# A macaron block on one core: the shared experts' work moved into the expert-pair loop, the experts' first layers computed transposed

## The reference, cut to what matters

```python
x = x + 0.5 * ffn(layernorm(x))
x = x + attention(layernorm(x))
x = x + 0.5 * ffn(layernorm(x))
def ffn(x):                                   # xf: (4096, 128)
    scores = softmax(xf @ gate_w.T)           # 64 experts, 6 chosen per token
    _, idx = top_k(scores + gate_b, 6)
    # the first 64 choices that fall on an expert, in token order, get a slot: xb (64, 64, 128)
    h = silu(einsum('ecd,eid->eci', xb, w1)) * einsum('ecd,eid->eci', xb, w3)   # i = 88
    yb = einsum('eci,edi->ecd', h, w2)
    y = scatter_add(yb * weight)              # back to the tokens
    z = (silu(xf @ ws1.T) * (xf @ ws3.T)) @ ws2.T    # shared experts, 176 wide
    return y + z
```

## Time and profile before

| what | value |
|---|---|
| median of 3 runs | 614.8 us (612.43 to 616.04) |
| the profiled execution's span | 615.3 us, mean granted TensorE clock 0.726 |
| busy | PE 448.7 us (73%), PEld 298.5 (49%), DVE 356.6 (58%), ACT 223.2 (36%), POOL 333.6 (54%) |
| first pass: loop, tail | POOL scatters from 103.3 to 184.0, planes added from 194.2 |
| attention | about 230 to 404 |
| second pass: loop, tail | POOL scatters from 494.0 to 574.7, planes added from 584.3 to 612.1 |
| chain that ended last | PE 32%, DVE 30%, DMA 12%, issue 12%, ACT 7%, POOL 4% |

### The profile page before, as it was taken

The page is one execution under the profiler, slowest core; times in us unless marked ns, Lnnn a source line. Parts: engine busy times, 40 slices in busy tenths (PEclk is TensorE's granted clock), DMA queues, the critical chain, the costliest instruction groups (busy, mean ns, idle before and its releaser), DMA issues.

```text
span 615.3 us, 12760 instructions
## 1 busy us (share of the span) xinstructions
PE 448.7 (73%) x4788; PEld 298.5 (49%) x4788; DVE 356.6 (58%) x992; ACT 223.2 (36%) x509; POOL 333.6 (54%) x259
## 2 busy tenths in 40 slices
PE   1876965996699425799999979147877399957970
PEld 1823643553345313577777768146445255524440
DVE  6497981221113992687777865487999232212097
ACT  4732112332224268555555530184321133312420
POOL 6177786888886700322222220003877678888691
PEclk9987785555559755799999986558778555555995
DMA  7988500101008990001111110541000000100592
GB/s 256 387 243 317 230 8 7 11 5 11 6 5 314 410 368 1 1 3 38 35 34 35 34 36 10 161 173 52 2 0 8 8 8 6 10 6 7 166 410 108
DMA packets 34388, 60.39 MB, mean 98 GB/s; under 512 B 12611, under 2 KB 18846, under 8 KB 33870
## 3 DMA queue, kind: packets, MB, share of 16 engines
q1 hardware_dynamic: 23078, 58.41, 26.5%
q0 software_dynamic: 11264, 1.38, 2.5%
HBM read 37.43 MB, written 29.36 MB: 109 GB/s over the span
## 4 chain that ended last, share of the span: by engine, by line
PE 32%; DVE 30%; DMA 12%; issue 12%; ACT 7%; POOL 4%; another core or an unknown queue 1%; SPq 1%; DVEq 0%; POOLq 0%; ACTq 0%
DVE X L971 9%; DMA rows_d<-A 5%; PE bank L776 5%; PE bank L895 5%; PE bank L793 4%; PE bank L876 4%; PE bank L766 3%; PE bank L786 3%; ACT A L508 3%; DMA planes_d<-Bb,put_i 3%; DVE Cb L1074 2%; DVE bn L976 2%; DMA Bb<-planes_d 2%; POOL planes_d L438 2%; DVE A L1055 2%
## 5 line engine op out<-in xcount | busy, mean ns | idle before, releaser
L438 POOL DMA_INDIRECT planes_d<-Bb,put_i x64 | 100.4, 1569 | 26.1 <-issue 19.4
L452 POOL DMA_INDIRECT A<-rows_d,tok_i x64 | 71.4, 1116 | 20.1 <-issue 16.6
L1104 DVE TENSOR_TENSOR ring<-ring,bank 128x88 f32<-128x88 f32 x64 | 15.8, 246 | 107.2 <-ACT ring L574 77.4
L673 PE MATMUL bank<-ident,A 128*128 128x128 f32 x96 | 21.6, 399 | 54.4 <-ACT A L508 40.2
L479 POOL TENSOR_TENSOR Bb<-Cb,chm 128x576 f32<-128x576 f32 x16 | 19.0, 1221 | 67.1 <-DVE Cb L1138 33.7
L396 POOL TENSOR_TENSOR Bb<-Eb,st 128x512 f32<-128x512 f32 x8 | 8.9, 1112 | 79.3 <-DVE st L1022 79.3
L766 PE MATMUL bank<-ident,A 128*128 128x128 f32 x64 | 29.8, 465 | 29.4 <-DMA A<-rows_d,tok_i 23.5
L703 PE MATMUL bank<-XT,ws1s 128*88 128x512 f32 x64 | 41.4, 734 | 6.2 <-DVE Eb L1016 5.3
L568 ACT ACTIVATE ring<-bank 128x128 f32<-128x128 f32 x64 | 17.8, 278 | 77.6 <-PE bank L766 67.0
L673 PEld LDWEIGHTS bank<-ident,A 128*128 128x128 f32 x96 | 17.4, 212 | 57.3 <-issue 29.9
L479 POOL TENSOR_TENSOR Bb<-w3s,chm 128x576 f32<-128x576 f32 x16 | 17.9, 1148 | 49.2 <-PE bank L918 49.2
(11 more groups left out here) (155 smaller groups left out, 1108.3 us busy)
## 6 DMA issues: line engine op xcount, KB each, us to landing
planes_d<-zeros SPq DMA_DIRECT2D x8, 2048.0 KB, 20.9
w3s<-in_w3T SPq DMA_DIRECT2D x2, 2816.0 KB
rows_d<-A SPq DMA_DIRECT2D x8, 512.0 KB, 12.4
A<-planes_d SPq DMA_DIRECT2D x8, 512.0 KB, 9.5
PL<-planes_d SPq DMA_DIRECT2D x8, 512.0 KB, 10.2
Cb<-planes_d SPq DMA_DIRECT2D x8, 512.0 KB, 10.9
Bb<-planes_d SPq DMA_DIRECT2D x8, 512.0 KB, 12.0
w1s<-in_w1T SPq DMA_DIRECT2D x1, 2816.0 KB
```

Source lines behind the costliest of these rows:

```text
L438: pool.indirect_dma_start(out=planes_d[f], in_=Y[:, s, :], in_offset=None, out_offset=bass.IndirectOffsetOnAxis(ap=put_i[:, s:s + 1], axis=0),
L452: pool.indirect_dma_start(out=A[:, t, :], out_offset=None, in_=rows_d, in_offset=bass.IndirectOffsetOnAxis(ap=tok_i[:, t:t + 1], axis=0), ...
L673: ins = pe.transpose(bank[g % 2][:, (i % 4) * P:(i % 4 + 1) * P], A[:, i, :], ident[:, :])
```

## The change

The experts' first layers are computed transposed: the weights are now the stationary operand (88 columns), the gathered slots XBT the moving one (64 columns per expert), and the output is 88 x slots. With it go `g_turn`, ACT's `copy_gT` and one step of the loop's skew: the gated product is written by DVE straight to where `expert_out` reads it.

All shared-expert work moves into the loop: iterations s = 2 to 25 each do one part, `shared_hidden(g, 0)`, `shared_hidden(g, 1)` or `shared_out(g)`, for g from 0 to 7. Hidden layers use banks 1 and 6, the output bank 1 again. ACT applies Silu from bank 1; DVE, no longer POOL, multiplies with bank 6 read from PSUM, and adds half of the output to X itself. The matmul of twice X and the constant for it go.

In the tail DVE adds all four planes; POOL has nothing to do there.

```diff
-    EARLY = 4
-    BASE_AFTER = EARLY - 2
...
+        SH = [PL[0:I, 512 * k:512 * k + 512] for k in range(2)]
+        HS = [[PL[0:I, 1024 + 512 * (2 * j + k):1536 + 512 * (2 * j + k)] for k in range(2)] for j in range(2)]
...
-        SHARED = ((0, 1), (4, 5))
+        SHARED = (1, 6)
+
+        def shared_part(s):
+            n = s - 2
+            return divmod(n, 3) if 0 <= n < 3 * NSH else None
...
-                sp.wait_ge(z_added, NSH * f + EARLY)
+                sp.wait_ge(z_added, NSH * (f + 1))
...
-                for g in range(EARLY):
-                    shared_gates(g)
-                    if g == BASE_AFTER:
-                        counts()
+                counts()
...
-                def add_planes(g):
...
+                def shared_silu(g, k):
+                    n = (f * NSH + g) * 2 + k
+                    act.wait_ge(sh_ps, n + 1)
+                    if n >= 2:
+                        act.wait_ge(sh_gated, n - 1)
+                    act.activation(SH[k], bank[SHARED[0]][0:I, :], ACT.Silu).then_inc(sh_silu, 1)
...
-                    act.activation(SG[s % 2], bank[2 + s % 2][:, 0:I], ACT.Silu)\
-                        .then_inc(silu_done, 1)
...
+                    act.activation(SG[s % 2], bank[2 + s % 2][0:I, 0:P], ACT.Silu).then_inc(silu_done, 1)
+
+                for s in range(NS + 2):
                     if s < NS:
                         copy_xbT(s)
                     if 1 <= s <= NS:
                         silu(s - 1)
-                    if 2 <= s <= NS + 1:
-                        copy_gT(s - 2)
-                shared(EARLY, NSH)
+                    part = shared_part(s)
+                    if part and part[1] < 2:
+                        shared_silu(*part)
...
                 def shared_hidden(g, k):
                     n = (f * NSH + g) * 2 + k
-                    if g == 0 and k == 1:
-                        pe.wait_ge(shifted, NG * (f + 1))
-                    if g == EARLY:
-                        pe.wait_ge(y_sb, (f + 1) * NS)
-                    if g:
-                        pe.wait_ge(sh_copied, 2 * (n - 1))
-                    for w, bk in zip((ws1s, ws3s), SHARED[k]):
+                    if g == 0 and k == 0:
+                        looked_up(6)
+                    if n:
+                        pe.wait_ge(sh_gated, n)
+                    if k == 0 and (f or g):
+                        pe.wait_ge(z_added, f * NSH + g)
+                    for w, bk in zip((ws1s, ws3s), SHARED):
...
                 def shared_out(g):
-
                     n = f * NSH + g
-                    if n:
-                        pe.wait_ge(z_added, n)
-                    pe.matmul(bank[7][:, :], twice[:, :], X[:, 4 * g:4 * g + 4, :].rearrange("p i d -> p (i d)"),
-                              start=True, stop=False, skip_group_check=True)
                     pe.wait_ge(sh_gated, 2 * n + 2)
...
-                    for w, off in ((w1s, 0), (w3s, I)):
+                    for w, off in ((w1s, 0), (w3s, P)):
                         for k in range(2):
-                            ins = pe.matmul(bank[2 + s % 2][CAP * k:CAP * k + CAP, off:off + I], XBT[s % 2][:, CAP * k:CAP * k + CAP],
-                                            w[:, 2 * s + k, :], start=True, stop=True)
+                            cols = slice(off + CAP * k, off + CAP * k + CAP)
+                            ins = pe.matmul(bank[2 + s % 2][0:I, cols], w[:, 2 * s + k, :],
+                                            XBT[s % 2][:, CAP * k:CAP * k + CAP], start=True, stop=True)
...
-                for s in range(NS + 3):
+                for s in range(NS + 2):
                     if s < NS:
                         xb_turn(s)
                     if 1 <= s <= NS:
                         hidden(s - 1)
-                    if 2 <= s <= NS + 1:
-                        g_turn(s - 2)
-                    if s >= 3:
-                        expert_out(s - 3)
...
+                    if s >= 2:
+                        expert_out(s - 2)
+                    part = shared_part(s)
+                    if part and part[1] < 2:
+                        shared_hidden(*part)
+                    elif part:
+                        shared_out(part[0])
...
-                    for buf in PLANES[0:3]:
-                        if buf is PLANES[2]:
-                            dve.wait_ge(planes_added, NG * (n // 2) + g + 1)
+                    for buf in PLANES:
                         then(dve.tensor_tensor(xg, xg, buf[:, cols], ALU.add))
...
-                    dve.tensor_tensor(GA[s % 2], SG[s % 2], bank[2 + s % 2][:, I:2 * I], ALU.mult).then_inc(gated, 1)
+                        dve.wait_ge(y_ps, f * NS + s - 1)
+                    dve.tensor_tensor(GT[s % 2], SG[s % 2], bank[2 + s % 2][0:I, P:2 * P], ALU.mult).then_inc(gated, 1)
+
+                def shared_gate(g, k):
+                    n = (f * NSH + g) * 2 + k
+                    dve.wait_ge(sh_silu, n + 1)
+                    if g >= 2:
+                        dve.wait_ge(z_ps, f * NSH + g - 1)
+                    dve.tensor_tensor(HS[g % 2][k], SH[k], bank[SHARED[1]][0:I, :], ALU.mult).then_inc(sh_gated, 1)
+
+                def shared_add(g):
+                    xg = X[:, 4 * g:4 * g + 4, :].rearrange("p i d -> p (i d)")
+                    dve.wait_ge(z_ps, f * NSH + g + 1)
+                    dve.scalar_tensor_tensor(xg, bank[SHARED[0]][:, :], 0.5, xg, ALU.mult, ALU.add).then_inc(z_added, 1)
```

More of the change, by code:

```diff
@@ L106, in macaron_kernel @@
         plane0 = sb("plane0", [P, NS])
-        twice = sb("twice", [P, P])
         gate_s = sb("gate_s", [P, NE])
@@ L189, in macaron_kernel @@
         counts_ready = sem("counts_ready")
-        sh_copied = sem("sh_copied")
+        sh_silu = sem("sh_silu")
         group_ready = sem("group_ready")
@@ L361, in _ @@
             pool.memset(eps[:, :], LN_EPS).then_inc(ident_ready, 1)
-            then(pool.memset(twice[:, :], 0.0))
-            keep(twice[:, :], ALU.not_equal, 0, [[-1, P]], 1, 2.0)
             then(pool.memset(before[:, :], 1.0))
@@ L456, in _ @@
                     add(s)
-                def add_planes(g):
-                    cols = slice(g * GI * D, (g + 1) * GI * D)
-                    pool.wait_ge(part_in[g], 16 + 64 * (f + 1))
-                    pool.tensor_tensor(out=PLANES[2][:, cols], in0=PLANES[2][:, cols], in1=PLANES[3][:, cols],
-                                       op=ALU.add).then_inc(planes_added, 1)
-                for g in range(EARLY, NSH):
-                    if g >= NSH - 2:
-                        add_planes(g - (NSH - 2))
-                    shared_gates(g)
-                for g in range(2, NG):
-                    add_planes(g)
                 if f == 0:
@@ L716, in shared_out @@
                         for k in range(2):
-                            ins = pe.matmul(bank[7][:, i * D:(i + 1) * D], SHARED_BUFS[g >= EARLY][2][g % 2][k][:, i * P:(i + 1) * P], ws2s[:, k, :],
-                                            start=False, stop=(k == 1), skip_group_check=True)
+                            ins = pe.matmul(bank[SHARED[0]][:, i * D:(i + 1) * D], HS[g % 2][k][:, i * P:(i + 1) * P],
+                                            ws2s[:, k, :], start=(k == 0), stop=(k == 1))
                     ins.then_inc(z_ps, 1)
@@ L737, in look_up @@
                             ins.then_inc(look_ps, 1)
[L739 to L752 removed]
+                base()
                 look_up()
[L754 removed]
                 pe.wait_ge(w_in, 48 + 16 * f)
@@ L1109, in weigh @@
                                       ALU.mult, ALU.mult).then_inc(y_sb, 1)
-                for s in range(NS + 3):
+                for s in range(NS + 2):
                     if 1 <= s <= NS:
                         gate(s - 1)
-                    if s >= 3:
-                        weigh(s - 3)
+                    if s >= 2:
+                        weigh(s - 2)
+                    part = shared_part(s)
+                    if part and part[1] < 2:
+                        shared_gate(*part)
+                    elif part:
+                        shared_add(part[0])
             ffn(0)
```

84 lines of the change are left out of this document (7 added, 77 removed).

## The result

The changed kernel took 628.1 us, median of 4 runs (626.25 to 632.96), against 614.6 us for the kernel before on the same chip (median of 4, 612.43 to 616.04): ratio 1.0228, 95% interval 1.0189 to 1.0267, 2.3% slower. Forecast were 612.9 us.

A forecast was written before the change was run, and what follows sets the result against it. GpSimd was taken to bound the expert loop, VectorE the tails; with the change TensorE's chain bounds the loop. Loops +5.1 and +4.3 us, tails -5.4 and -6.4: -2.4 on 615.3, so 612.9 us, range 595 to 640.

The forecast's parts named there:

- What bounds the kernel: Before the change: GpSimd's gathers and scatters set the expert-pair loop's end, VectorE bounds after the last scatter.
- the chain of a hidden iteration: Expert loop: TensorE's hidden part plus wait for VectorE's product, 3.38 us, becomes the bound; 3.02 after an output part.
- Which clock: Expert loop: half clock for the first two or three iterations, 1.7 us more, then full clock until the parts end.
- The second rival: Expert loop: clock stays low, a hidden iteration takes 5.7 us; a quarter of the pairs gives 640 us; chance 0.23.
- Late completions at the loop's entrance: Loop's start: ScalarE learns late of finished matmuls; counted 1.0 us, since first shared parts run inside those waits.
- The sum: Whole kernel: loops +5.1 and +4.3 us, tails -5.4 and -6.4, together -2.4 us, giving 612.9 us.
- The third rival: Loop's start: late completions lie on the path, some 9 us a pass; half of that gives 620.9 us; chance 0.14.
- Ahead of the loop: Before the first gathers: less GpSimd work beside VectorE saves 1.1 us in the first pass, 1.9 in the second.
- Parts' end to last scatter: Loop's end, first pass: the last scatter starts 16.6 us after the shared parts end, at 187.5 us.
- Tails: After the last scatter: VectorE alone adds, 1.22 us an addition; saves 5.4 us in the first pass, 6.4 in the second.

The follow-up runs named there:

- warm: Changed kernel with 23 more 512-column matmuls a pass between the look-ups ahead of the loop, raising the clock: 619.1 us, ratio 1.0146 to the kernel before.
- turned: Kernel before with only the experts' first layers transposed, without gated transpose and its copy; shared work and tails as before: 611.0 us against 610.1, ratio 0.9999.

## Why the prediction was wrong

- **What bounds the kernel; the chain of a hidden iteration.** Right: 3.35, 3.35, 3.07 us for 3.38, 3.38, 3.02, a pair 2.17 and 1.20 us for 2.2 and 1.23.
- **Which clock.** Right for the settled part of the loop, and on B for the entrance: full clock until the parts end, and half clock costs 0.6 and 1.4 us there instead of 1.7. Wrong for the entrance on the opening chip, see the next point. The second rival, a clock that swings through the whole loop, didn't come: it rested on the rule in the Trainium skill, TensorE: Matmul & The Clock Gate, section on psum-queue depth-cycling. The rows of chip B show TensorE waiting 0.32 us for VectorE's product in two of three parts and granted 1.00 throughout; the trace does not bear the rule out here.

```profile
106.90:164.50 57.60, 53.80 (x370) 35.63 (x368) 20.45 (x53) 14.60 (x47) 41.52 (x31) 1.00 0.07 6
```

- **Late completions at the loop's entrance, and the clock there: the step that failed.** The sum took 1.0 us a pass for them, "since the first shared parts run inside those waits". They don't: each part needs three signals in turn (matmul to ScalarE, to VectorE, to TensorE), so a late first one stops the next part. Forecast for the entrance were 19.5 + 1.7 + 1.0 = 22.2 us; 31.5 and 31.05 were measured, 18.2 us over. 612.9 + 18.2 = 631.1 against 628.1; the parts begin earlier than forecast (86.4 for 90.9 us in the first pass), which hides a part of the loss. In the two opening profiles the last scatters come 11.0 and 11.8 us later than before, where 5.1 and 4.3 were forecast. The third rival named the mechanism and the full price, "some 9 us a pass", and then took half of it, at a chance of 0.14. The earlier trace rows had shown them, and no row spoke for 1.0. What no row of one profile could show is that some chips have them and others not.

  The stops are only half of the loss. The entrances of both passes, opening chip and then B (length, then busy time of PE, PEld, DVE, ACT and POOL, then the granted clock):

```profile
86.37:117.87 31.50, 26.57 (x128) 16.84 (x126) 7.48 (x18) 5.44 (x17) 19.32 (x16) 0.72 0.06 7
484.11:515.16 31.05, 23.34 (x128) 15.31 (x127) 7.40 (x18) 5.40 (x17) 19.32 (x16) 0.80 0.07 8
...
86.75:106.90 20.15, 18.88 (x128) 12.38 (x126) 6.92 (x18) 5.03 (x16) 16.18 (x14) 0.97 0.09 11
470.81:491.79 20.98, 19.71 (x129) 12.59 (x127) 6.92 (x18) 5.04 (x16) 16.71 (x14) 0.93 0.09 11
```

  The same six parts keep TensorE busy 18.27 us of 19.54 when all are at full clock (`warm`). So half clock cost 8.3 and 5.1 us on the opening chip, 10.0 more than the 3.4 in the sum, and standing still 3.7 and 6.4 us, 8.1 more than the 2.0 in it (estimates from these busy times). Both terms of the entrance were undersized, the clock's no less than the signals'. That the late signals kept the clock down is likely, since the first six parts are granted 0.67 to 0.81 in every profile of such a loop with late signals and 0.89 or more in every one without; no run separates the two.
- **Ahead of the loop.** Undersized: the slots are done at 84.6 instead of 89.9 (1.1 us forecast, 5.3 found; with this stage unedited they are done at 87.2 on chip A and 89.5 on C, so a part of it may not be the change); in the second pass, counted from its first statistics, after 79.7 us instead of 83.7 (1.9 forecast, 4.0 found). The scan, one row, now takes 4.42 us in both passes.

```profile
L963 DVE TENSOR_TENSOR_SCAN A<-Eb x2: 4424/4424/4425, 51.5 to 449.2; 128x2048 f32<-128x2048 f32 x2
```

- **Parts' end to last scatter.** 16.6 us forecast, 18.1 found.
- **Tails.** Right against the kernel before on the opening chip: 5.6 and 7.0 us for 5.4 and 6.4, with 1.22 us an addition. Their cause was told too simply; see the table of tails. The rule of the Trainium skill, SBUF — State Buffer, section Who interferes with whom, agrees with the rows: of the kernel before and `turned`, an addition that starts in the midst of a GpSimd product or addition takes 2.1 to 5.6 us, and one that stands alone 1.22.
- **The sum where no signal is late.** The transposed kernel has the loop and tails of before and its time (0.9999); its profile (chip A) and that of the changed kernel (B) compare so: last scatter 176.84 and 182.90, +6.1 (forecast +5.1); tail 33.1 and 29.7, -3.3 (-5.4); from the second pass's first statistics to its last scatter 173.4 and 176.0, +2.5 (+4.3); tail 28.2 and 20.9, -7.3 (-6.4). Together -2.0 us, forecast -2.4. Measured were -0.2% and -0.4%, forecast -0.4%. That the sums agree so well is partly luck: single terms are off by 1 to 2 us with opposite signs, and executions of one kernel on one chip differ by more than the whole sum.

## What to carry to other kernels

Moving work under another engine's bound turns a loop with slack into one where each stage waits for the last; price its start by every stall seen there before, at full, since the slack that hid them is what the change spends, and add what a stop-and-go start costs at half clock. Where two engines come out nearly even, the order counts: the same 24 parts in three of four iterations rather than in a row were worth 2.1 to 2.6% on the chips where signals are in time. On E, with the second pair of banks beside it, nothing clear was left of that. And a change of this size is measured on more than one chip before it is kept.

## What the runs showed of the hardware

- TensorE's completion signals can arrive late and in order: in the opening profile the matmuls that end by 91 us are signalled at 97.1, the output matmuls started at 90.85 at 99.2, and those due at 95.8, 96.0 and 97.2 within 0.2 us of that. TensorE itself runs on meanwhile. Late by 3.7 us or more, it happens at the fourth or fifth pair of each loop (in most by 1.4 us or more at one or two pairs before or behind it as well), on the opening chip, C and E in all 8 profiles, on A, B and D in none of 12. Its cause stays open: no instructions are loaded between 80 and 100 us of the opening profile, and the burst of gathers wasn't varied on a chip that has it.
- The clock stays at its upper level (2.4 GHz, granted 1.00) with TensorE busy 53.8 of 57.6 us in stretches broken by waits of 0.32 us, and at the lower one (1.2 GHz, 0.50) with 65.65 of 88 us, in the kernel without parts:

```profile
88.00:176.00 88.00, 65.65 (x392) 51.15 (x390) 19.36 (x61) 17.49 (x60) 71.52 (x54) 0.50 0.08 7
```
